# GpSimd waits for the landing of each tile's gathers before it issues the next tile's

## The reference

```python
# 1. deformable attention on a 32 x 32 grid of query points of each image
q_feat  = bilinear_sample(feature_map, grid_points)           # [B, 1024, 64]
queries = q_feat @ W_q.T
h       = gelu(layer_norm(q_feat @ W_o1 + b_o1))
points  = grid_points + (h @ W_o2 + b_o2) * 4 * scale         # 8 points of each query
sampled = bilinear_sample(feature_map, points)                # [B, 1024, 8, 64]
k, v    = sampled @ W_k.T, sampled @ W_v.T
out     = softmax over the 8 points of (q . k / sqrt(8)), times v, for each of 8 heads
# 2. a class token is put ahead; h + attn(layer_norm(h)), where attn is a recurrence
#    over the 1025 positions (running maximum, two running sums), its output gate,
#    and a gated feed-forward block
# 3. h + moe(layer_norm(h)): each token goes through the one of 32 small experts
#    that its router scores highest
```

## Time and profile before

| what | value |
|---|---|
| timed runs, median (lowest to highest) | 2933.29 us (2933.29 to 2938.32) |
| span of the profiled execution | 3729.2 us |
| last gather issued, profiled execution | 3546.5 us |
| GpSimd busy, profiled execution | 2145.8 us in 2048 gathers |
| TensorE, VectorE, ScalarE busy | 2549.7, 2323.3, 1343.0 us |
| mean granted TensorE clock | 0.841 |

### The profile page before, as it was taken

How to read it: one execution, slowest core, us unless ns; L and a number is a source line. 1 busy time by engine, 2 the same in 40 slices (tenths; PEclk the granted TensorE clock), 3 DMA queues, 4 the chain that set the end, 5 groups by cost and what they waited for, 6 DMA issues and landing times.

```text
span 3729.2 us, 33872 instructions
## 1 busy us (share of the span) xinstructions
PE 2549.7 (68%) x10680; PEld 1648.7 (44%) x10680; DVE 2323.3 (62%) x3092; ACT 1343.0 (36%) x2326; POOL 2145.8 (58%) x2052
## 2 busy tenths in 40 slices
PE   2556767676586757758676675757667675776788
PEld 2434445444454445434444443434445443444443
DVE  3655767575576757657675666757657675666661
ACT  1323333343333324323342333324333342433364
POOL 5564666566476656656566475646657566566600
PEclk6778888888798888879887897878878888888899
DMA  4232323323233232322323232222322323232300
GB/s 142 75 96 72 96 84 89 88 87 100 74 88 92 87 91 86 98 80 79 93 84 98 72 103 77 85 86 86 94 85 82 92 85 98 81 86 82 84 10 11
DMA packets 139226, 314.68 MB, mean 84 GB/s; under 512 B 68912, under 2 KB 69296, under 8 KB 134960
## 3 DMA queue, kind: packets, MB, share of 16 engines
q0 software_dynamic: 98304, 268.57, 25.0%
q1 hardware_dynamic: 40880, 45.58, 3.7%
HBM read 305.62 MB, written 8.40 MB: 84 GB/s over the span
## 4 chain that ended last, share of the span: by engine, by line
DVE 35%; another core or an unknown queue 31%; PE 16%; issue 12%; ACT 5%; DVEq 0%; DMA 0%; ACTq 0%; SPq 0%
DVE weighed L1044 8%; PE work_ps L472 5%; DVE scores L1079 4%; PE points_ps L513 3%; DVE products L1072 3%; DVE scores L1059 3%; DVE products L1056 2%; PE work_ps L494 2%; PE work_ps L573 2%; PE kv_ps L525 1%; PE work_ps L603 1%; DVE state_p L1117 1%; DVE state_q L1114 1%; DVE state_o L1104 1%
## 5 line engine op out<-in xcount | busy, mean ns | idle before, releaser
L457 POOL DMA_INDIRECT gathered<-pixels,index x2048 | 2145.6, 1048 | 1401.4 <-DVE weighed L1044 732.0
L707 ACT ACTIVATE sampled_t<-points_ps 128x512 f32<-128x512 f32 x256 | 153.3, 599 | 1456.8 <-remote 858.2
L525 PE MATMUL kv_ps<-kv_sb,sampled_t 128*128 128x256 f32 x2048 | 513.0, 405 | 206.9 <-issue 166.9
L513 PE MATMUL points_ps<-c_sb,weighed 128*128 128x128 f32 x4096 | 540.4, 289 | 139.7 <-DVE weighed L1044 126.4
L513 PEld LDWEIGHTS points_ps<-c_sb,weighed 128*128 128x128 f32 x4096 | 503.9, 151 | 253.6 <-DVE weighed L1044 162.1
L1044 DVE TENSOR_TENSOR weighed<-gathered,mix 128x1024 f32<-128x1024 f32 x512 | 600.2, 1213 | 8.2 <-remote 6.5
L525 PEld LDWEIGHTS kv_ps<-kv_sb,sampled_t 128*128 128x128 f32 x2048 | 407.0, 203 | 305.9 <-issue 199.2
L1056 DVE TENSOR_TENSOR products<-kv_ps,queries 128x1024 f32<-128x1024 f32 x128 | 156.1, 1219 | 448.2 <-remote 417.8
L472 PE MATMUL work_ps<-hn,w_sb 128*128 128x512 f32 x544 | 316.1, 705 | 159.5 <-ACT wide L772 106.6
L1072 DVE TENSOR_TENSOR products<-kv_ps,probs 128x1024 f32<-128x1024 f32 x128 | 156.2, 1220 | 368.1 <-ACT probs L712 350.3
L603 PE MATMUL work_ps<-nm,w_sb 128*128 128x512 f32 x544 | 283.0, 602 | 8.3 <-DVE xm L1207 6.0
(11 more groups left out here) (167 smaller groups left out, 3308.9 us busy)
## 6 DMA issues: line engine op xcount, KB each, us to landing
grid_px<-grid SPq DMA_DIRECT2D x32, 1024.0 KB
gathered<-pixels,index POOLq DMA_INDIRECT x2048
out<-rm SPq DMA_DIRECT2D x32, 256.0 KB
w_sb<-weights SPq DMA_DIRECT2D x1, 1984.0 KB, 8.9
moe_hidden<-consts SPq DMA_DIRECT2D x1, 512.0 KB, 9.8
attended<-cls SPq DMA_DIRECT2D x1, 512.0 KB, 11.5
c_sb<-consts SPq DMA_DIRECT2D x1, 192.0 KB, 5.1
w_sb<-weights SPq DMA_DIRECT2D x1, 192.0 KB, 5.1
```

What stands on the lines that cost most here:

```text
L457: pool.indirect_dma_start(gathered[:, n % RING, k * PATCH:(k + 1) * PATCH], None, pixels, bass.IndirectOffsetOnAxis(ap=index[:, n // TILES ...
L513: mm = pe.matmul(points_ps[:, j * P:(j + 1) * P], weighed[:, n % 2, at:at + 2 * C], ident, is_transpose=True, start=(q == 0), stop=(q == 3))
L525: mm = pe.matmul(kv_ps[:, 2 * (n % 2) + j // 2, (j % 2) * 2 * P:(j % 2 + 1) * 2 * P], sampled_t[:, n % 2, j, :], kv_sb[:, :], start=True, ...
```

## The change

Before it issues the eight gathers of a tile, GpSimd also waits until all eight gathers of the tile before have landed. For tiles 1 to 15 of an iteration this is the count that the tile before brings its slot's semaphore to, the same count for which `weigh` waits; for tile 0 it is the count at the end of the iteration before (none in iteration 0). Nothing else differs.

```diff
                     pool.wait_ge(weighted.sem, weighted.at(it, n - RING + 1))
 
+                    if n > 0:
+                        before = slot_gathered[(n - 1) % RING]
+                        pool.wait_ge(before.sem, before.at(it, ((n - 1) // RING + 1) * HEADS * 16))
+                    elif not isinstance(it, int) or it > 0:
+                        before = slot_gathered[RING - 1]
+                        pool.wait_ge(before.sem, before.at(it, 0))
+
                     pool.sem_inc(tiles_started.sem, 1)
                     for k in range(HEADS):
                         at = (n % TILES) * HEADS + k
                         pool.indirect_dma_start(
```

## The result

The changed kernel takes 3560.48 us (median of 4 runs, 3559.69 to 3563.14), the kernel before 2933.53 us beside it. The ratio is 1.2137, 95% interval 1.2122 to 1.2152: 627 us slower. The forecast was 3420 us, so the direction and the mechanism held, and the size was short by 140 us, half a microsecond outside the range.

The account below looks back on a forecast made before the run. GpSimd's gathers, issued end to end, were taken to bound the kernel. 2933 + 510 for 255 exposed landings - 38 for VectorE delays + 15 for grid loads = 3420 us (chance 0.73); 8-in-10 range 3230 to 3560.

Parts of the forecast that it names:

- What bounds the kernel: GpSimd's gathers, issued end to end, set the time at 10.64 us a tile; TensorE needs 9.34, VectorE 8.74.
- a looser GpSimd: Rival: timed GpSimd issues at 1.25 us a gather, leaving 164 us of slot waits to use up; 3280 us, chance 0.12.
- a wait hidden in the slot waits: Rival: GpSimd's slot waits, 732.0 us in the profile, cover the landing; time stays at 2933 us, chance 0.05.
- The chain without waits: GpSimd's gathers from first to last, slot waits and stops taken out: 2760 us for 256 tiles, 10.78 each.
- The wait is never free: At each of 255 tile boundaries GpSimd waits from its eighth issue's end until the landing is seen; 510 us added.
- The landing, 1.80 us from issue to a reader's start: Read from VectorE's start after tile 1's last gather; last byte 1.4 us after issue end, VectorE's start at 1.80.
- How fast GpSimd comes back: After a wait GpSimd begins 0.57 us later than another engine; gap between tiles taken as 2.30 us, bounds 1.80 to 2.60.
- The 38 us off for VectorE's instructions that fall into waits: Of 208 us by which VectorE instructions delay gathers, the share falling into GpSimd's waits delays nothing: 38 us taken off.
- the 15 put for grid loads: Grid loads or stores filling the DMA engines make about 12 exposed landings later: 15 us added, bounds 0 and 192.
- The page's price: Skill's rule for a GpSimd-issued DMA: 2.0 us plus bytes at 436 GB/s, 2.30 us to semaphore; 655 us added in all.
- TensorE's clock: Rival: TensorE, waiting more, falls to its lower clock more often; 358 us added, half of it about 3600; chance 0.07.
- The profiled span: Changed kernel's profile grows far less than its time, slot waits absorbing most of 510 us; span 3750 to 4000 us.

Follow-up runs that it names:

- lag2: Changed kernel, but GpSimd waits before tile n for the landing of tile n-2 in place of n-1; 2934.04 us, ratio 1.0007 to the kernel before.
- even: Changed kernel with the wait only before tiles of even number, 127 waits in place of 255; 3246.66 us, ratio 1.1074 to the kernel before.
- twice: Changed kernel with a second wait in each tile, before the fifth gather for the first four; 4118.14 us, ratio 1.4014 to the kernel before.
- later1: Changed kernel with the wait after the tile's first gather instead of before it; 3256.45 us, ratio 1.1105 to the kernel before.
- seven_after: Changed kernel with seven gathers a tile in place of eight, the eighth fetched only in the first four tiles; 3232.25 us.

## Why the prediction was right in kind and short in size

- *What bounds the kernel.* Right, and shown twice; with it the rivals of a looser GpSimd and of a wait hidden in the slot waits are out. The 732 us of slot waits were not in the timed kernel: lag2 has 0.3 us of them. The chain without waits, 2760 us, was 15 us above lag2's 2745; the tail of 181.7 was 14 above its 167.5.
- *The wait is never free, and nothing hides it.* Right: even, with half the waits, costs half (315 of 627 us).
- *The landing, 1.80 us from issue to a reader's start.* Right: 1.83 in the changed kernel, the last byte at 1.4 in both. Some luck is in it. In the earlier trace rows VectorE was busy until 50.59 and started at 50.90, after the same 0.30 us of idle time that it has before its instruction at 48.24, which waited for no landing. A landing up to 0.3 us earlier would have given the same row.
- *How fast GpSimd comes back.* This is the step that failed. The rows had it at 0.80 us after VectorE's end, 0.57 more than TensorE needs. I took a gap of 2.30, on the ground that the 1.80 already holds VectorE's own start, so that 0.50 of the 0.80 was all I added. It does not: where VectorE is idle it starts 0.02 us after the last count (median), so the 1.80 is the landing alone, and GpSimd's 0.79 stands whole behind it. Measured: 0.76 after VectorE, a gap of 2.58. The upper bound, 2.60, was the right reading. Of the 140 us missed, (2.58 - 2.30) x 255 = 71 are this step.
- *The 38 us off for VectorE's instructions that fall into waits.* Wrong in this kernel, and worth 36 of the 140 us: GpSimd's busy time is 2119.2 us against lag2's 2121.0. The lower busy time than in the recording before (2145.6) would have looked like a confirmation; that recording held 25 us more than lag2's. The term has no fixed size: against lag2 the delays are 2 us less in the changed kernel, 18 less in even, 46 less in twice and 15 more in later1, and with seven gathers the wait takes 35 us off. They move with where the gathers fall beside VectorE's work, and a share of the idle time doesn't tell that. By the Trainium skill's rule on the port (SBUF — State Buffer, "SBUF: two separate sides") one would expect delays only beside certain instructions of VectorE. That the total moves while VectorE's own busy time stays (2258 and 2257 us in the stretch) agrees with it, but no run tests it.
- *A term that was missing.* At every twelfth tile the gap before the second gather was 1.88 us where it should be 0.30 (1013.24 above, and 1166.02, below); 21 of these are 33 us. So the sum is (2.62 - 0.30) x 255 = 591, + 33, - 2 = 622 us, against 487 forecast. The late landings are in the 2.62: (2.62 - 2.58) x 255 = 10 us, against the 15 put for grid loads. Of the 140 us missed, 71 + 36 + 33 - 5 = 135 are thus named.
- *The page's price.* The estimate from the Trainium skill (DMA: Bandwidth & Descriptors, "Anatomy of one DMA — SWDGE (gpsimd) path") gave 655 us, nearer to 627 than my 510. It put 2.30 us from issue to semaphore, where this trace has 1.79. The return of 0.57 that I added to it is too short against 0.79, so the two parts miss on opposite sides, and that the sum comes near is luck.
- *TensorE's clock.* The granted clock fell from 0.93 to 0.87 and TensorE's busy time in the stretch rose from 2301.5 to 2473.1 us, as the rival said; at 13.15 us a tile (3366.29 / 256) there was room, and the gaps of GpSimd alone make 623 of the 627 us. Seven_after agrees: against the changed kernel GpSimd's busy and idle time fell by 329 us (3366.3 without the first wait to 3037.5), and the time by 328.
- *The profiled span*, forecast at 3750 to 4000, was 3559.1. I had taken the idle stretches of one recording for a habit of every recording.

## What to carry to other kernels

A wait for a DMA that the same engine has just issued costs its whole landing and the engine's own return, each time, if that engine sets the time; the same wait one stage older is free. Here that was 2.46 us against nothing for one tile more in flight, and two gathers issued ahead of the wait (2.50 us) already hid all but the late landings. When an idle engine's return from a wait has a row of its own, use it whole rather than discount it: here it was 0.80 us after VectorE's end and 0.785 after the last count of a DMA.

## What was not expected

At every twelfth tile (14, 26 and so on to 254), that is every 96 gathers, something holds the gathers up by 1.6 to 2.4 us, but only in kernels that wait for a landing near it. In the changed kernel it is a gap of 1.88 us before the second gather (here again, twelve tiles after 1013.24):

```profile
1163.20 0.94 POOL L464 DMA_INDIRECT gathered<-pixels,index  x1 [2.62 <-issue]
1166.02 1.78 POOL L464 DMA_INDIRECT gathered<-pixels,index  x1 [1.88 <-issue]
```

and in later1 the gap of 3.61 us in place of 1.3, with no load on the DMA engines to explain it. The landing is not late there: its last count comes 1.7 us after the issue's end, as at other tiles, and GpSimd starts 3.14 us after the count in place of 0.80. lag2 shows none. In seven_after the same pause comes at every fourteenth tile (20, 34 and so on), every 98 gathers, which is about as many gathers but two tiles more. So it goes by the number of gathers and not by tiles or iterations. What recurs was not found.
